# Transformer layer on one core: z and q by way of DRAM, two relu parts on DVE, low parts on POOL, new orders

## The reference

```python
q = x @ Wq + bq; k = ctx @ Wk + bk; v = ctx @ Wv + bv      # per head, 16 columns each
scores = q k^T / 4, masked: key j is seen by query i only where j < i
attn = softmax(scores), row of query 0 set to 0
x1 = layer_norm(x + (attn v) @ Wo + bo) * g1 + b1n
out = layer_norm(x1 + relu(x1 @ W1 + b1) @ W2 + b2) * g2 + b2n
```

## Time and profile before

| | us |
|---|---|
| runs, median (lowest to highest) of 3 | 1664.52 (1663.47 to 1664.58) |
| profiled execution, whole | 1664.95 |
| profiled execution, span of the trace | 1663.1 |
| PE / DVE / ACT / POOL busy in it | 1622.1 / 1434.9 / 1545.7 / 1379.0 |
| mean granted clock of PE | 0.985 of full |

### The profile page before, as it was taken

How to read it: one execution, slowest core, us unless ns; L and a number is a source line. 1 busy time by engine, 2 the same in 40 slices (tenths; PEclk the granted TensorE clock), 3 DMA queues, 4 the chain that set the end, 5 groups by cost and what they waited for, 6 DMA issues and landing times.

```text
span 1663.1 us, 54091 instructions
## 1 busy us (share of the span) xinstructions
PE 1622.1 (98%) x16700; PEld 1595.2 (96%) x16700; DVE 1434.9 (86%) x6744; ACT 1545.7 (93%) x5907; POOL 1379.0 (83%) x1352
## 2 busy tenths in 40 slices
PE   4799999999999999999999999999999999999997
PEld 4799999999999999999999999999999999999997
DVE  3688898898898898898898898898898898898885
ACT  3799999999999999999999999999999999999993
POOL 2378888888888888888888888888888888888896
PEclk7799999999999999999999999999999999999999
DMA  8856656656656655656665666655666666765530
GB/s 152 168 120 124 130 134 122 131 126 128 132 135 119 133 133 119 133 133 119 135 136 115 136 131 119 135 134 118 134 135 119 132 133 121 132 135 121 120 69 27
DMA packets 307087, 208.99 MB, mean 126 GB/s; under 512 B 164336, under 2 KB 281968, under 8 KB 306800
## 3 DMA queue, kind: packets, MB, share of 16 engines
q1 hardware_dynamic: 305104, 204.60, 59.8%
q10 hardware_dynamic: 1696, 0.92, 0.3%
HBM read 104.73 MB, written 50.33 MB: 93 GB/s over the span
## 4 chain that ended last, share of the span: by engine, by line
PE 95%; DVE 2%; ACT 1%; SPq 1%; DMA 1%; issue 1%; POOL 0%; POOLq 0%; ACTq 0%; DVEq 0%
PE ps_dense L386 32%; PE ps_dense L397 32%; PE ps_probsT L493 14%; PE ps_scores L483 7%; PE ps_att L511 7%; PE ps_dense L368 2%; ACT probs L588 0%; DVE ps_scores L795 0%; PE ps_att L410 0%; DMA probs<-in_L_xattn_Wk_dram 0%; DMA q_stack<-qT 0%; SPq L240 0%; SPq L246 0%; SPq L262 0%; SPq L283 0%
## 5 line engine op out<-in xcount | busy, mean ns | idle before, releaser
L588 ACT ACTIVATE probs<-ps_scores,negmax 128x128 f32<-128x128 f32 x2048 | 741.7, 411 | 8.6 <-DVE negmax L795 5.1
L1046 POOL TENSOR_TENSOR probs<-probs,recip 128x512 f32<-128x512 f32 x512 | 530.9, 1037 | 136.6 <-DVE recip L778 136.5
L795 DVE CUSTOM_DVE_ANT_0 ps_scores<-ps_scores,mask 128x128 f32<-128x128 f32 x2048 | 527.1, 318 | 71.6 <-PE ps_scores L483 69.3
L588 ACT ACTIVATION_READ_ACCUMULATOR probs<-ps_scores,negmax 128x1 f32 x2048 | 515.4, 252 | 0.0
L397 PE MATMUL ps_dense<-w,hT 128*128 128x256 f32 x3048 | 418.0, 286 | 0.9 <-DVE u L920 0.9
L386 PE MATMUL ps_dense<-zT,w 128*128 128x256 f32 x3072 | 416.9, 285 | 0.8 <-DVE h_f L879 0.5
L1054 POOL TENSOR_TENSOR hT<-h_f,hT 128x512 fp32r<-128x512 f32 x252 | 321.2, 1284 | 90.3 <-DVE h_f L879 90.3
L386 PEld LDWEIGHTS ps_dense<-zT,w 128*128 128x128 f32 x3072 | 381.8, 189 | 1.5 <-issue 0.9
L397 PEld LDWEIGHTS ps_dense<-w,hT 128*128 128x128 f32 x3048 | 377.5, 188 | 1.2 <-DVE u L920 1.1
L605 ACT ACTIVATE probsT<-ps_probsT 128x508 f32<-128x508 f32 x512 | 318.7, 623 | 39.5 <-PE ps_probsT L493 39.5
L493 PE MATMUL ps_probsT<-ident,probs 128*128 128x128 f32 x2048 | 313.8, 275 | 0.0
(11 more groups left out here) (92 smaller groups left out, 2350.1 us busy)
## 6 DMA issues: line engine op xcount, KB each, us to landing
k_stack<-k_spill SPq DMA_DIRECT2D x384, 128.0 KB, 4.4
q_stack<-qT SPq DMA_DIRECT2D x762, 64.0 KB, 2.0
k_spill<-kT SPq DMA_DIRECT2D x128, 256.0 KB, 2.2
c_tok<-in_ctx_dram SPq DMA_DIRECT2D x256, 64.0 KB, 4.8
x_res<-in_x_dram SPq DMA_DIRECT2D x64, 256.0 KB, 3.2
x_tok<-in_x_dram SPq DMA_DIRECT2D x252, 64.0 KB, 2.4
out_dram<-o_tok SPq DMA_DIRECT2D x63, 256.0 KB, 2.7
probsT<-in_L_xattn_W_dram SPq DMA_DIRECT2D x1, 1024.0 KB, 11.0
```

What stands on the lines that cost most here:

```text
L588: last = nc.scalar.activation(probs[:, m % 4, i, :], ps_scores[m % 2][:, i, :], ACT.Exp, bias=negmax[:, m % 4, i:i + 1], scale=-1.0, accum ...
L795: last = nc.vector.tensor_tensor_reduce(ps_scores[m % 2][:, i, :], ps_scores[m % 2][:, i, :], mask[:], -1.0, -MASKED, ALU.add, ALU.min, ac ...
L1046: nc.gpsimd.tensor_tensor(probs[:, m % 4], probs[:, m % 4], recip[:, m % 4, :].unsqueeze(2).broadcast_to([P, 4, S]), ALU.mult)\
```

## The change

What it does:

- **z through DRAM.** `z_transpose` and its bank are gone. SP stores `u1` (`spill_z`) and loads it back in blocks of 32 rows (`load_z`, 4 DMAs) into the tile of `x_res`, which is free between the residual sum and the next residual load; DVE flips it in place (`z_flips`), ACT rounds it and POOL subtracts.
- **q through DRAM.** As k: 2 spills and 3 loads a group in place of 12 copies. Group 0 keeps the direct copies.
- **Relu of f1_1 and f1_3 on DVE alone.** max(u + b1, 0) = max(u, -b1) + b1: the high part is max(u, -b1) rounded, the low part max(u, -b1) less the high part, both from PSUM. The missing b1 is constant over tokens, so its product with W2 is added once to the offset row of norm 1 (`fold_shift`, four float32 matmuls at group 1; `fold_rows`). f1_0 and f1_2 go as before.
- **Low parts** of x and the context from DVE to POOL (except group 0).
- **Orders** of all five engines, banks and `HELD_BY` are new. v is projected one group ahead; Wv and Wo are loaded and split before the first scores; the last group's norm 2 is done by DVE and POOL per sequence, and its second half stored from ACT.

The diff, cut to its core:

```diff
-ITERATIONS = range(-5, NG + 6)
+SHIFTED = (1, 3)
+ITERATIONS = range(-4, NG + 6)
-BANK = {"zT": 2, "v": 0, "q": 2, "f1_0": 2, "k": 0, "f1_1": 1, "f1_2": 2, "f1_3": 0, "wo": 1, "f2": 1}
+BANK = {"v": 1, "q": 1, "f1_0": 0, "k": 2, "f1_1": 1, "f1_2": 0, "f1_3": 1, "wo": 2, "f2": 0}
+HELD_BY = {"f1_3": ("f1_1", 0), "q": ("f1_3", 5), "v": ("q", -1), "f1_1": ("v", -3), "f2": ("f1_2", 0),
+        "f1_0": ("f2", 1), "f1_2": ("f1_0", 0), "k": ("wo", 3), "wo": ("k", -2)}
...
+            def spill_q(g, part):
+                if exists(g) and g > 0:
+                    if part == 0:
+                        sp.wait_ge(s_hi["q"], KC * (g + 1))
+                    else:
+                        sp.wait_ge(taken["q"], KC * (g + 1))
+                    need(sp, s_qstack, 16 * PARTS * (g - 2))
+                    sp.dma_start(q_dram[g % 2, part].rearrange("c p t -> p c t"), f32(qT[:, part])).then_inc(s_qspill[part], 16)
+            def stack_q(g, part):
...
+                            sp.dma_start(f32(q_stack[g % 2][32 * s:32 * s + 32]), q_rows[g % 2, part]).then_inc(s_qstack, 16)
...
             def load_residual(g):
-                    need(sp, taken["wo"], g)
+                    need(sp, s_zlo, g)
                     sp.dma_start(x_res[:], x_v[g]).then_inc(s_xres, 16)
+            def spill_z(g):
+                if exists(g):
+                    sp.wait_ge(s_z1, GB * (g + 1))
+                    need(sp, s_zrow, 16 * 4 * (g - 1))
+                    sp.dma_start(z_dram[g % 2].rearrange("b s d -> s b d"), u1[:]).then_inc(s_zspill, 16)
+            def load_z(g):
+                if exists(g):
+                    sp.wait_ge(s_zspill, 16 * (g + 1))
+                    sp.wait_ge(taken["wo"], g + 1)
+                    for j in range(4):
+                        sp.dma_start(z_tile[32 * j:32 * j + 32], z_blocks[g % 2, j]).then_inc(s_zrow, 16)
...
             def iteration(it):
+                spill_k(it + 2, 1)
+                next_x(it + 4)
                 stack_k(it + 2, 0)
+                load_residual(it)
+                stack_k(it + 2, 1)
+                spill_q(it + 3, 0)
+                store(it - 3)
                 next_c(it + 4)
+                spill_q(it + 3, 1)
+                spill_z(it)
                 stack_q(it + 3, 0)
-                load_residual(it + 1)
+                spill_k(it + 3, 0)
+                load_z(it)
                 stack_q(it + 3, 1)
-                spill_k(it + 3, 0)
-                spill_k(it + 3, 1)
-                store(it - 2)
-                next_x(it + 5)
-                stack_k(it + 3, 1)
```

```diff
+            def h_shifted(g, n):
+                if exists(g):
+                    dve.wait_ge(full[f"f1_{n}"], g + 1)
+                    need(dve, full["f2"], g)
...
+                    for i in range(2):
+                        ch = 2 * n + i
+                        nc.vector.tensor_scalar(hT[:, 0, ch, :], ps_dense[BANK[f"f1_{n}"]][:, i * GT:(i + 1) * GT],
+                                                neg_b1[:, ch:ch + 1], None, ALU.max).then_inc(s_hshift, 1)
+                    for i in range(2):
+                        ch = 2 * n + i
+                        dve.wait_ge(s_hshift, done + i + 1)
+                        last = nc.vector.scalar_tensor_tensor(
+                            out=hT[:, 1, ch, :], in0=ps_dense[BANK[f"f1_{n}"]][:, i * GT:(i + 1) * GT],
+                            scalar=neg_b1[:, ch:ch + 1], in1=f32(hT[:, 0, ch, :]), op0=ALU.max, op1=ALU.subtract)
+                    last.then_inc(taken[f"f1_{n}"], 1)
+            def z_flips(g):
+                if exists(g):
+                    dve.wait_ge(s_zrow, 16 * 4 * (g + 1))
+                    nc.vector.transpose(z_tile, z_tile).then_inc(s_zflip, 1)
+            def z_lo(g):
+                if exists(g):
+                    pool.wait_ge(s_hi["zT"], g + 1)
+                    nc.gpsimd.tensor_tensor(zT[:, 1].rearrange("p c (o t) -> p c o t", t=32), z_by_chunk(),
+                                            f32(zT[:, 0]).rearrange("p c (o t) -> p c o t", t=32), ALU.subtract)\
+                      .then_inc(s_zlo, 1)
+            def last_norm():
...
+                    dve.wait_ge(s_lnm, b + 1)
+                    nc.vector.scalar_tensor_tensor(out=u2[:, b, :], in0=u2[:, b, :], scalar=neg_mean[:, 1, b:b + 1],
+                                                   in1=g2_row[:], op0=ALU.add, op1=ALU.mult).then_inc(s_lgain, 1)
+                for b in range(GB):
+                    dve.wait_ge(s_lrs, b + 1)
+                    dve.wait_ge(s_lgain, b + 1)
+                    nc.vector.scalar_tensor_tensor(out=u2[:, b, :], in0=u2[:, b, :], scalar=rstd[:, 1, b:b + 1],
+                                                   in1=be2_row[:], op0=ALU.mult, op1=ALU.add).then_inc(s_lout, 1)
```

More of the change, by code:

```diff
@@ L382, in columns_product @@
                     bank_free(g, name)
+                if g == 1 and BANK[name] == BANK["v"]:
+                    pe.wait_ge(taken["v"], 1)
                 for i, ch in enumerate(chunks):
@@ L412, in fold_offset, with fold_shift @@
                 last.then_inc(s_fold, 1)
-            def z_transpose(g):
-                if exists(g):
-                    pe.wait_ge(s_z1, GB * (g + 1))
-                    transposes(g, "zT", u1)
+            def fold_shift():
+                pe.wait_ge(s_w[5], 16 * len(RAW[5]))
+                pe.wait_ge(s_b1wide, 1)
+                for n, ch in enumerate(SHIFTED_CHUNKS):
+                    raw, c, _ = RAW[5][ch // GB]
+                    last = nc.tensor.matmul(ps_att[:, 0:D], b1_wide[:, n], raw[:, ch - c],
+                                            start=(n == 0), stop=(n == len(SHIFTED_CHUNKS) - 1))
+                last.then_inc(s_fold2, 1)
             def q_project(g, first=False):
@@ L450, in ff_up @@
                 if exists(g):
-                    pe.wait_ge(taken["zT"], g + 1)
+                    pe.wait_ge(s_zlo, g + 1)
                     weights_split(g, 4)
@@ L482, in scores @@
                     c, j = w // 2, 2 * (w % 2) + i
-                    last = nc.tensor.matmul(bank[:, 2 * i:2 * i + 2, :], q_stack[g % 2][:, j, c, b * S:(b + 1) * S],
+                    last = nc.tensor.matmul(bank[:, 2 * i:2 * i + 2, :], q_stack[g % 2][:, 4 * c + j, b * S:(b + 1) * S],
                                             k_stack[g % 2][:, 4 * c + j, :, b * S:(b + 1) * S], start=True, stop=True)
                 last.then_inc(s_scores, 1)
+                if g == 1 and m == 1:
+                    fold_shift()
             def probs_transpose(g, m):
```

423 lines of the change are left out of this document (233 added, 190 removed).

## The result

The changed kernel takes **1687.53 us** (median of 4 runs, 1686.44 to 1690.49), the kernel before 1664.47 us beside it: ratio 1.0141, 95% interval 1.0129 to 1.0154. It is 23 us slower. The forecast was 1633.

What follows compares the result with a forecast made beforehand. TensorE was taken to bound the kernel: 1664.95 us less 28.2 for z's transposes and 3.2 for the new order, plus 0 for the edges, gave 1633.5; forecast 1633 us, range 1624 to 1652.

Steps and rivals of the forecast that it cites:

- The edges: Start and tail of the run: gains and losses there come together to 0, from -7 to +9 us.
- Do the others fit: Middle, per group: ACT 22.0, DVE 22.3 and POOL 22.8 us all stay under the new period of 24.38.
- Does the new order hold: Middle: everything fits at 24.38 us, nothing by much; DVE's 0.9 us of waits for TensorE soak up lateness.
- The bound: Whole kernel: whatever TensorE no longer does is gained, as long as the other engines fit under the shorter period.
- z's 0.44 us: TensorE, each group: removing z's four transposes gains 0.44 us, x64 = 28.2 us.
- The new period of 24.38: TensorE, each group: 24.87 us less 0.44 for z's transposes and 0.05 for the order.
- Three blocks instead of two now precede an L397 block: gain 0.05: TensorE's new order: a block costs 1.37 us before an L397 block, otherwise 1.42; 0.05 a group, 3.2 us in all.
- scores behind a transposition: TensorE, seven places a group: scores take 0.32 us, the extra 0.08 moving from block to scores; bounds 0.56 either way.
- z's landing: Middle: z's load taken at 10 us, up to 11.8 unpunished; rival, landing at 13.2 gives 1722 us, chance 0.09.
- -5 for the blocks: Start: half-filled early groups lose five blocks that TensorE was late with; -5 us, bounds 0 and -9.
- The rewritten last norm: Tail: drops ACT's pass, one DVE pass and the wait for both halves; -2.7 us.
- The last z's detour: Tail: the last z's way through DRAM takes 13.5 us against 10 us of cover; +4 us.

Runs made afterwards that it cites:

- e4: The kernel before with only one of z's four transpositions per block left in place: 1644.57 us, 0.9878.
- g2: g1 and f6 together, so the changed kernel with columns cut and POOL's residual sum later: 1671.41 us, 1.004; period 24.513.
- e5: The changed kernel without z's way through DRAM (spill and four loads left out): 1690.95 us, 1.0158; period 25.014.
- g1: The changed kernel with DVE's 128x2 column instructions of the moments cut into 128x1: 1674.37 us, 1.0051; period 24.626.
- c1: The changed kernel with the edits of g1, e1b and e2 together: 1671.26 us over 10 runs, 1.0038; period 24.545.
- f6: The changed kernel with POOL's residual sum one normalisation later: 1696.28 us, 1.0186; period 25.000.
- t1: s1 without z's way through DRAM (spill and four loads left out): 1653.95 us, 0.9929; period 24.513.
- s1: g2 with the start reordered in full (x(1) ahead of splits; q's and k's traffic ahead of W2 and rows): 1655.79 us, 0.9943.
- a1: The changed kernel with its start reordered as in s1, nothing else: 1679.42 us, 1.0086; period 24.881.
- c2: c1 with a first reordering of the start (splits, loads and spills): 1667.95 us, 1.0017; period 24.583.
- e1b: The changed kernel with q's low part ahead of norm 2's moments in DVE's order: 1680.01 us, 1.0086; period 24.654.
- e2: The changed kernel with z in its own tile, rows of bo and g2 replaced by those of bv and g1: 1679.9 us, 1.0081.
- e3: The changed kernel with SP's start-up loads of rows, W1 and W2 put behind q's and k's traffic: 1683.91 us, 1.0112.

## Why the prediction was wrong, by its own steps

Three steps of it failed, in this order of size: "The edges" had no term for what the new queue and split order do to the start (the start came 21.3 us later than forecast, +18.8 for -2.5); "Do the others fit" and "Does the new order hold" left DVE's small column instructions and a forced wait of POOL out (16.5 us in the middle); and the sum of TensorE's slots was too short (8 us). The tail adds 6.5.

**The bound, and z's 0.44 us.** Right. e4 shows TensorE's time flowing through, and in g2 the new order runs at its slots.

**The new period of 24.38.** The sum of TensorE's slots was 0.13 short: they come to 24.51. "Three blocks instead of two now precede an L397 block: gain 0.05" was the failing term. The row had 1.37 us for one such pair, v and f2; in the new order f1_0 to v, v to wo and f1_3 to f2 all take 1.41. One row had been made a rule; three times 0.04 is most of the 0.13. The term that looked riskier, scores behind a transposition, took 0.32 as forecast, the blocks behind them 1.41 to 1.44. Over 60 groups the 0.13 is 8 us: the middle could gain 21.3 (1490.7 - 1469.4 in g2), not 29.

**"Do the others fit".** POOL 22.8 forecast; 226.19 over 10.03 periods is 22.6. Right in size. ACT 22.0, measured 22.6. DVE 22.3 forecast, 22.9 measured, and the column instructions (+1.03 a group) more than account for the excess; I had left them inside the old sum because they were small. **This is the step that failed in the middle.** The prediction read the port conflict only for the large instructions with two SBUF inputs, and concluded that taking these off DVE makes POOL less likely a bound. For those it held: DVE's no longer slow POOL (its y_b sum went from 1732 to 1290 ns). But a 128x2 instruction is held while one of POOL's large instructions (1.04 to 1.29 us) runs, and POOL now has more of them (22.6 us a group for 21.5) at other moments. How much is the added work and how much the new order was not separated; with POOL's work all but unchanged, the columns take from 1.91 (after) to 2.52 us (e5), so the order has a large share. The old trace could have said that there was something to count. Its groups of the same stretch:

```profile
L908 DVE TENSOR_SCALAR var_eps<-mv 128x2 f32<-128x2 f32 x100 | 28.0, 280 | 3.6 <-DVE mv L905 0.2
...
L909 DVE TENSOR_SCALAR neg_mean<-mv 128x2 f32<-128x2 f32 x100 | 15.8, 158 | 0.0
```

Two instructions of one shape, 280 and 158 ns: the first was held even then. In 50 of its 100 places it takes up to 393 ns and ends 27 to 29 ns behind a POOL instruction, and in the other 50 it takes 0.17 us.

**"Does the new order hold".** I gave DVE some 0.9 us of waits to soak up lateness before q's low part; up to 2.1 us of held columns stand just ahead of it (439.44 to 441.56 above). Cutting them gives back 0.17 of the 0.28 us between 24.80 and 24.51 (g1); the other 0.11 goes with POOL's order, with the residual's load landing in 5.1 us (g2), though c1 gets 0.08 of it without touching that order, by q's low part ahead and z's own tile. I had forecast POOL's spare 1.6 us, but not that 1.84 us of forced waiting at one place of an in-order queue would take it. POOL's wait is no bound by itself: f6 took most of it away with a loss, and POOL then waited for DVE instead.

**z's landing.** Right. Its load lands in 2.6 us, DVE waits 0.3 us a group for it (15.6 in 50), and leaving the detour out gains nothing in the middle (e5, t1). The pieces of 256 B, for which I had cited the Trainium skill (DMA: Bandwidth & Descriptors, Specifications) as a rival, show no doubling here: 2.6 against the 2.4 of x. x is loaded in the same pieces, so what longer pieces would take no run shows. The DMA share is 0.75 of 24.8, 18.6 us, below the 21 forecast.

**The start, forecast +2.5 for fold_shift and -5 for the blocks, measured +18.8.** The largest miss. I priced fold_shift (2.5; its rows take 3.1 us, 70.92 to 73.98) and the blocks, and had no term for SP's queue or for splits that stand ahead of x(1). s1 shows it: of the 21.1 us by which g2's start is longer than before, 16.5 were the order of loads, splits and spills; in the changed kernel the same reordering gives 11.6 (a1). Some part belongs to the splits ahead of x(1); s1 undid both together, so how much is the queue's alone stays open. For the queue speaks c2, with the splits moved but rows and W2 at other places, which had come 9.7 us later than s1 (it has e1b's and e2's edits besides); against it e3, which moved only SP's loads and gained nothing. The clock plays in as well: from 40 to 80 us its mean grant is 0.58 in g2, 0.70 in the changed kernel and 0.78 in s1, and no run separates it. Of the five blocks that the start was to lose, two went (240 matmuls of dense blocks ahead of scores(3, 0) before, 216 after).

**The tail, forecast net +2.3, measured +8.8.** The rewritten last norm: from the last matmul to the end 5.4 us (1680.49 to 1685.9; forecast 4.4, before 7.1), so -1.7. The last z's detour, forecast +4, shows in TensorE's rows of after:

```profile
1655.76 5.91 PE L463 MATMUL ps_dense<-w,hT 128*128 128x256 f32 x48
1665.33 8.99 PE L452 MATMUL ps_dense<-zT,w 128*128 128x256 f32 x48 [3.66 <-POOL zT L1166]
```

TensorE stands for 3.7 us until POOL has z's low part, and the next 48 matmuls take 8.99 us where the 48 before took 5.91. Their mean granted clock is 0.65 (1665.33 to 1674.32), and 1.00 in the stretch before the wait; in the wait the clock had fallen to the lower level, 1.2 GHz. Together that is 6.8 us for the 4 of the forecast, and e5, without the detour and at full clock there, has a tail 6.5 us shorter. Here a wait near the end cost nearly twice its length. Not forecast either: the new order runs the feed-forward products later, so that behind scores(63, 0) stand 372 matmuls of the dense blocks, where before had 348. That is two blocks of 1.42, 2.8 us, less 1.7 for three transpositions of z and one of probabilities fewer. They are the two that the start no longer has. With 1.5 us more of small waits of TensorE for other engines the terms come to 7.7 of the 8.8; the rest is open, and g1, whose edit is in the form alone, has a tail of 68.0.

**Summed up.** -29.4 forecast in the middle (0.49 x 60); 8 us of it was never there, 16.5 were lost to held columns and POOL's order; the start lost 19 and the tail 9. The experiments recover the middle (g2) and most of the start (s1). Whether the remaining 4.6 us of s1's start (113.0 against 108.4) come from the low clock and the softmax chain of the first groups was not tried. The direction of the whole was no bad luck either: the middle, had it run at its slots, would have gained 21.3 us, and the start and the tail of the changed kernel lose 27.6. g2, which has such a middle, is slower than the kernel before (1.004).

## What to carry to other kernels

Where DVE and GpSimd both work from SBUF, look at the mean of the smallest DVE instructions by form: one that takes several times what its neighbour of the same size takes may be held, and is where its end follows another engine's each time. Its idle time is counted as busy, and here another form, one column at a time, cured it even at twice the instructions. When a change moves work to GpSimd, count what it does to those as well as to the large ones. And forecast the start by SP's queue, instruction by instruction, as the steady state is forecast: an unchanged middle can lose to twenty loads in front of the first spill.

## What the runs showed of the hardware that was not expected

- A 128x2 tensor_scalar on DVE took up to 1.33 us beside a running POOL instruction and 0.15 us where it was cut to 128x1. A reciprocal of 128x4 beside them stayed at 160 ns, and the transposition of 128x512 at 690.
- W2's split on DVE (two SBUF inputs, 128x512) took 1.41 (mean of two) and 1.75 us beside POOL and 0.68 once alone.
- Taking work away can make this pipeline slower: e5 without the detour 0.22 us a group, f6 without most of a wait 0.20, both with more time in DVE's held columns (2.52 and 2.36 us a group for 1.91).
- TensorE's clock fell to its lower level during a wait of 3.7 us near the end, and the 48 matmuls behind it took 8.99 us for 5.91.
